# Attention's products with the values: one block in every slot, or two blocks in every second slot

## What is computed

```python
scores = jnp.einsum('bhqk,bhsk->bhqs', q, k) / jnp.sqrt(jnp.float32(dk))
scores = jnp.where(causal_mask, jnp.float32(-1e9), scores)
weights = jax.nn.softmax(scores, axis=-1)
ctx = jnp.einsum('bhqs,bhsk->bhqk', weights, v)
concat = ctx.transpose(0, 2, 1, 3).reshape(b, s, d)
return concat @ Wo + bo
```

## Time and profile before

| | |
|---|---|
| runs, us | 1681.05, 1685.39, 1686.82 |
| span of the profiled execution, us | 1684.0 |
| attention's slots in it, us from the start | 960 to 1471 |
| PE busy | 1346.8 us (80%) |
| DVE busy | 1232.3 us (73%) |
| ACT busy | 895.3 us (53%) |
| POOL busy | 916.5 us (54%) |

### The profile page before, as it was taken

The page is one execution under the profiler, slowest core; times in us unless marked ns, Lnnn a source line. Parts: engine busy times, 40 slices in busy tenths (PEclk is TensorE's granted clock), DMA queues, the critical chain, the costliest instruction groups (busy, mean ns, idle before and its releaser), DMA issues. The chain is left out here.

```text
span 1684.0 us, 25407 instructions
## 1 busy us (share of the span) xinstructions
PE 1346.8 (80%) x7325; PEld 726.0 (43%) x7325; DVE 1232.3 (73%) x2340; ACT 895.3 (53%) x1660; POOL 916.5 (54%) x746
## 2 busy tenths in 40 slices
PE   6848888888888989999536899999899998822756
PEld 2313333333333378999523344443343343211743
DVE  6999999999998643252576988889889888260324
ACT  5746666566665645566324166655555565701423
POOL 1479889999897037352642012113463455674773
PEclk9879999999999979999868899999999999955877
DMA  1029100000000045787506212111221113311317
GB/s 56 0 68 343 38 0 0 0 0 0 0 0 0 1 113 165 200 231 203 140 21 211 60 31 57 34 31 31 75 62 35 39 43 77 79 18 45 102 52 251
DMA packets 121420, 122.69 MB, mean 73 GB/s; under 512 B 29778, under 2 KB 96575, under 8 KB 118904
## 3 DMA queue, kind: packets, MB, share of 16 engines
q1 hardware_dynamic: 99404, 97.47, 20.7%
q0 software_dynamic: 10240, 15.79, 3.3%
q10 hardware_dynamic: 11660, 8.01, 1.6%
HBM read 76.68 MB, written 50.52 MB: 76 GB/s over the span
## 5 line engine op out<-in xcount | busy, mean ns | idle before, releaser
L1962 ACT ACTIVATE t_PT<-t_ps_s 128x1024 f32<-128x1024 f32 (+3 forms) x384 | 294.2, 811 | 229.5 <-PE t_ps_s L2271 228.4
L1984 DVE TENSOR_REDUCE t_negm<-t_ps 128x1 f32<-128x512 f32 (+4 forms) x624 | 368.6, 640 | 59.7 <-PE t_ps L2252 30.9
L464 POOL TENSOR_TENSOR s_HC<-s_H,X 128x1024 f32<-128x1024 f32 x128 | 307.1, 2417 | 40.0 <-DVE s_H L585 31.0
L629 PE MATMUL ps_y<-s_HC,ident 128*128 128x512 f32 x512 | 268.4, 649 | 20.9 <-POOL s_HC L464 19.4
L2252 PE MATMUL t_ps<-heads 128*128 128x512 bf16 (+3 forms) x768 | 233.8, 341 | 34.8 <-DVE t_negm L1984 21.6
L1896 POOL TENSOR_SCALAR_AFFINE_SELECT t_PT<-t_PT 128x512 f32<-128x512 f32 x128 | 84.4, 659 | 310.7 <-ACT t_PT L1962 310.4
L2271 PE MATMUL t_ps_s<-heads 128*128 128x512 bf16 (+3 forms) x768 | 180.9, 329 | 3.8 <-ACT t_PT L1962 2.1
L2286 PE MATMUL t_ps_c<-t_PT,t_VG 128*32 128x512 f32 (+3 forms) x1536 | 164.3, 501 | 1.1 <-ACT t_CT L1924 0.6
L525 ACT ACTIVATE s_dA<-m_DT,s_A 128x512 f32 (+1 forms) x192 | 127.5, 712 | 59.1 <-DVE s_H L585 58.2
L2252 PEld LDWEIGHTS t_ps<-heads 128*128 128x128 bf16 x768 | 73.3, 99 | 198.3 <-DVE t_negm L1984 142.4
L629 PEld LDWEIGHTS ps_y<-s_HC,ident 128*128 128x128 f32 x512 | 97.0, 201 | 124.1 <-issue 68.7
(11 more groups left out here) (337 smaller groups left out, 2368.5 us busy)
## 6 DMA issues: line engine op xcount, KB each, us to landing
f_w<-in_W_dram SPq DMA_DIRECT2D x93, 256.0 KB, 5.3
heads<-token_expert_rows SPq DMA_DIRECT2D x8, 1024.0 KB, 12.7
token_expert_rows<-X SPq DMA_DIRECT2D x42, 192.0 KB, 2.7
heads<-q_parts SPq DMA_DIRECT2D x42, 192.0 KB
heads<-k_parts SPq DMA_DIRECT2D x14, 576.0 KB
expert_rows<-X SPq DMA_DIRECT2D x27, 192.0 KB, 2.4
f_XS<-expert_rows SPq DMA_DIRECT2D x19, 256.0 KB
expert_rows_out<-f_YB ACTq DMA_DIRECT2D x19, 256.0 KB
```

The source lines that it names most:

```text
L464: nc.gpsimd.tensor_tensor(HC[:, g % RING], H[:, g % RING], row_wide(C_sb[:, g % RING, :], 2), ALU.mult).then_inc(s_hc, 2)
L629: nc.tensor.matmul(ps_y[c][:], ident[:], HC[:, g % RING, c, :], start=g == 0, stop=g == N - 1, skip_group_check=True).then_inc(s_y, 1)
L1962: nc.scalar.activation(PT[:, n % RP, 2 * p:2 * p + 2, 0:wd], src, ACT.Exp, scale=DK ** -0.5).then_inc(s_exp, 1)
L1984: nc.vector.tensor_reduce(out, ps_1[use % BANKS1][:, 0:h * width].rearrange("p (h k) -> p h k", h=h), AX.X, ALU.max, negate=True).then_inc ...
```

## The change

PE issues the product no longer in every slot but only in the odd ones, and there for two blocks: the one three slots back and the one two slots back. So the product of an even block stays in its slot and that of an odd block moves one slot ahead. The tail behind the last group has two products instead of three, since block 9 of the last group is now issued in slot 11. No instruction is added or removed on the other engines, and their order stays.

```diff
                         if x < 2:
                             scores(gi, n, x)
-                        elif x == 2 and gi * NB + n >= LAG:
-                            product((gi * NB + n - LAG) // NB, (n - LAG) % NB)
+                        elif x == 2 and n % 2 and gi * NB + n >= LAG:
+                            for back in (LAG, LAG - 1):
+                                product((gi * NB + n - back) // NB, (n - back) % NB)
...
-            for n in range(LAG):
-                product(TG - 1, NB - LAG + n)
+            for n in range(LAG - 1):
+                product(TG - 1, NB - LAG + 1 + n)
```

## The result

The changed kernel took 1699.32 us (median of 4 runs, 1697.84 to 1701.50), before 1683.42 us (4 runs on the same chip): ratio 1.0089, 95% interval 1.0068 to 1.0110. That is 15.9 us slower by the medians and 15.0 by the ratio.

The account below looks back on a forecast made before the run. PE was taken to bound nine groups, DVE's routing five, the scores-exponential chain two. 1684.0 + 6.6 + 2.5 + 3.7 = 1696.8, plus the span's 1.4 shortfall, said as 1697; own range 1690 to 1704, 8 in 10: 1682 to 1710.

Parts of the forecast that it names:

- What bounds: Attention: PE sets the pace in the first kind, DVE's routing in the second, the scores-exponential-scores chain in the third.
- first kind: Nine groups (0 to 4, 7, 8, 11, 12) paced by PE: each 0.73 us longer, 6.6 us in all.
- third kind: Groups 14 and 15, paced by scores and exponentials: scores behind two quartets make ACT stand, +3.7 us.
- second kind: Five groups (5, 6, 9, 10, 13) paced by DVE's routing work: +0.5 us a group, +2.5 us.
- The saving: Product quartets: each merged pair saves a 0.24 us edge; 94 places, at most 22.6 us; 1.44 a first-kind group.
- the waits of 2.17 us: New waits in a first-kind group: 1.56 us in slots 4 to 11, the others in slots 0 to 3.
- DVE's idle time: DVE's idle time before L1984 was to rise from 52.8 us by some 25 us.
- the first: Rival 1, chance 0.11: edges are won and the waits don't come, 13.0 plus 3.6 us saved, 1667 us.
- The second: Rival 2, chance 0.14: saving and waits of 1.44 cancel in first-kind groups, none more elsewhere, 1684 to 1687 us.
- The third: Rival 3, chance 0.12: longer PE waits bring group 5's clock fall to groups 9 and 13, 1709 us.
- The fourth: Rival 4, chance 0.03: the second quartet keeps its 0.24 us edge, nothing saved, waits stay, 1719 us.
- The rule of the Trainium skill on the tiling mode: Changing tiling mode drains the engine; by it alone all 94 merged pairs return their edge, 22.6 us, 1661.

Follow-up runs that it names:

- light covers: Maxima over a quarter of the columns: old order 1633.57 us, pairs 1638.29; exponentials cut to a quarter as well: old order 1627.42, pairs 1608.38.
- narrow pairs: Against the kernel before, only blocks 2 and 3 and blocks 10 and 11 paired: 1696.48 us, ratio 1.0075; with POOL's bias addition moved too, 1683.08, ratio 0.9998.
- both light: DVE's maxima and ACT's exponentials over only a quarter of the columns: order before 1627.42 us (ratio 0.9673), pairs 1608.38 us (ratio 0.9575).
- the addition moved: All pairs, with POOL's output-bias addition moved from behind the mask of block 3 to behind that of block 8: 1696.66 us, ratio 1.0087 against before.

## Why the prediction was right

1697 us was forecast, 1699.32 measured; +12.8 was the sum, +15.9 the difference.

- *What bounds*: right for the first and the third kind. The kernels with light covers show that PE sets the pace in the first kind and what holds it, and that ACT's exponentials make the loss of the third. What the second kind loses by was argued, and no run isolates it.
- *The saving*: right to the hundredth in groups 1 to 3, 1.44 us for six edges, when both covers are light. Over all 94 edges 22.6 us were put and about 17 shown.
- *First kind*: 6.6 us laid out, 6.3 measured by the copies, and this closeness is partly luck. The sum gave all nine groups 0.73 us. Groups 1 to 3 grew by 0.47, group 0 became 0.38 shorter, and groups 4, 7, 8, 11 and 12, whose other work was not laid out, grew by 0.8 to 1.3; the errors cancel. In groups 1 to 3 the laid-out slots 4 to 11 were right: 21.05 us put, 21.01 measured, with DVE's stand in slot 7 put at 1.39 and measured at 1.40. What was too high were slots 0 to 3, put at 9.05 and measured at 8.83 (8.92 before). So the waits of 2.17 us measured 1.91. The waits named step by step for slots 4 to 11 add up to 1.43, not to the 1.56 of the sum; the slots' length goes with the 1.56.
- *Second kind*: mis-sized. 2.5 us were put, 4.15 measured (0.32 to 1.18 a group), inside the bounds given; with the meeting taken out of both orders it is 6.2.
- *Third kind*: 3.7 us, measured 3.65 by the last copy, and 3.4 by the kernel that pairs only there (interval 0.5 to 6.4). Its parts are right too: slots 4 to 11 of group 14 were put at 17.45 us and took 17.60. With light exponentials the same stretch, from the last copy to the last product, becomes 0.6 us shorter by the pairs instead.
- *DVE's idle time*: put at 25 us more, measured 14.1 more (52.8 to 66.9). Part of what I counted as new idle time had been idle before: DVE's 1.40 us behind the pair of blocks 4 and 5 stand against 0.54 behind block 4 before.
- *Outside the sum*: the sum leaves out the 1.05 us that lie ahead of the attention's first scores and the 0.7 behind its last product. The attention itself, from first scores to last product, grew by 14.1 us where 12.8 were put.
- *Rivals*: the first falls, since its condition (waits under 1.44) held with real work in group 0 alone. The second falls with the waits of 1.91 and the interval of the ratio. The third named the fall of the clock in group 5 and put it down to longer waits of PE; it didn't spread to groups 9 and 13 with this change, and what makes PE stand there turned out to be the meeting of L2065 and L1892. It did spread with the narrow pairs. The fourth falls by the kernels with both light. The rule of the Trainium skill on the tiling mode (TensorEngine Tiling (Array Packing), Key Properties) agrees with a price of 0.24 us around a quartet, and the gain that it alone would give did not come. That the mode is the reason of the price is not shown: quartets differ from their neighbours also in type and in number of matmuls, and the turn of the maxima, one 32-column fp32 matmul between 128-column ones, has no such gap. In the timeline before, it starts 0.06 us behind a matmul of 128 columns, and the scores follow 0.10 later:

```profile
1049.29 0.22 PE L2255 MATMUL t_ps<-c_mask,c_identb 128*128 128x128 bf16 x1
...
1049.35 0.27 PE L2262 MATMUL t_ps<-ident,t_negm 128*32 128x128 f32 x1
...
1049.45 0.49 PE L2271 MATMUL t_ps_s<-heads 128*128 128x384 bf16 x2
```

Open: why the second kind loses what it loses, group by group; and the 0.7 us behind the last product. The times behind the last product run from 211.8 to 214.9 us over all profiles, and the four longest, the changed kernel's 214.1 among them, are those in which the stretch at a granted clock of 0.50 there lasts 78.5 us (75.1 before). Why it lasts longer is not shown.

## What to carry to other kernels

A fixed cost at each change between two kinds of work on the busiest engine can be real and still not be worth removing: batching makes bursts, and between the bursts slots in which the busiest engine runs ahead of the others. Before batching, check both. Compare the burst with what the rings hold (here 1.96 us against 3 banks, 1.83 us). And compare the slot that lost its work with what its consumer needs: PE had about 1.5 us of work in slot 6 where two exponentials take 1.82 us. A short burst alone is not enough, as the narrow pairs show; no pairing that was tried with the full work gained more than the spread of the runs. To learn what hides a saving, lighten one consumer at a time and look at the period of the loop.

## What the runs showed of the hardware

DVE's normalising instruction (fp32, SBUF to SBUF, per-partition scalars) stood while POOL ran a two-input addition: one of 32 took 2392 ns, the median is 337, and the addition lasted 2.34 us. DVE's instruction ended 0.08 to 0.09 us behind the end of the addition each time that the two met. With the narrow pairs one took 3.18 us: it had started 0.72 us ahead of the addition, while an indirect DMA of POOL (L1880) ran, so the addition may not be the only thing that it waited for. DVE's maxima from PSUM were not seen to stretch so: the longest beside an addition took 0.69 us.

A meeting put 2.1 to 4.3 us on a group. The least is the kernel with pairs in groups 0 to 13, whose granted clock stayed at 1.00 (41.59 us against 39.53 with the addition moved); the most is the kernel before (41.43 against 37.13), where the granted clock was 1.00 before PE's stand of 2.73 us and 0.50 (1.2 of 2.4 GHz) after it. Whether the two meet depends on little: in group 9 DVE had been done 0.65 us before POOL began. So a small edit elsewhere can move the total by 10 us: a miss of that kind is found by looking at every instance of a line, not at its mean.
